# Layer 2 of an attention kernel in another order of slots

## The chip, the cores and the metric

The kernel runs on one core of a Trainium2 chip. The metric is the time of one execution on the device in microseconds (us). The engines are TensorE (PE in the profile; its weight loads PEld), VectorE (DVE), ScalarE (ACT), GpSimd (POOL) and SyncE (SP), which here only issues transfers.

## The reference

Input x has 8 batches of 512 rows by 512 columns, float32.

```python
x = layernorm(x + attention_1(x))       # q, k, v, o each with a low-rank adapter; rope; causal; 16 heads of 32
x = layernorm(x + ffn(x))
# ffn: a = attention_2(rmsnorm(x, ln1_w)); mod = 0.1 * tanh(a @ A); h = rmsnorm(x, ln2_w)
# gate = silu(h @ W_in.T + mod * (h @ A) @ B); out = x + (gate * (h @ W_up.T)) @ W_down.T
```

## The kernel before

The program has three parts, one behind the other: layer 1 (attention 1, to 788 us of the profiled execution), layer 2 (output projection of attention 1, residual, layer norm, RMS norm, attention 2 with values narrowed to 16 columns a head; 788 to about 1690 us), and the MLP. Products of float32 numbers are made of three passes over high and low parts ("split": ScalarE writes the high part, VectorE or GpSimd subtracts it for the low part).

Layer 2 goes through 8 batches; a batch has 4 group steps (g0 to g3) of 4 heads; a step has 12 slots, three for each head. In slot k of step g of batch b, each engine does its share of a fixed program, written out by hand:

- TensorE (`step`, L2142): the transposed scores of unit k (`score_t_unit`, L275 and L277), the probabilities times values of unit k-2 (`pv_unit`, L311), in slots 1 to 7 one or two score units of the next group for its row maxima (`score_unit`, L192), and then what the slot has in extras.
- ScalarE: two exponentials of unit k (`exp_unit`, L286, L287), copies of PSUM results, and the send of the shift row.
- VectorE: the low part of the probabilities of unit k-1 (`lo_unit`, L294, always first in the slot), the maxima (`score_max`, L206), in slot 7 `shift_split` (L217, L219), in slot 5 the reciprocal of the sums (`invert`, L1915), and extras.
- GpSimd: sums of the attention outputs (`merge` L1578, `weigh` L1584 to L1599), two of the four row tiles of h (`normalise_tile`, L1615), splits of the next attention output (`attn_chunk`, L1603).
- SyncE: gathers, stores, loads, and `stack_send` (L258, L262), twelve transfers for a group that bring q and k into the layout that the scores need.

`score_t_unit(k)` waits for `lo_done` of unit k-2, since its PSUM buffer has two halves. On VectorE that subtraction opens slot k-1.

The extras prepare batch b+1 during batch b. Their order: the output projection (`project_out`, L2067 and L2072, 52 matmuls, four tiles of rows, slots from `OUT_SLOTS` and `OUT_COUNT`) into the two halves of `lin_ps`; `add_residual` (L1846, with its statistics L1848); `variances` (L1855 to L1863), the roots by Newton steps (`root_start` L1307, `root_round` L1315 to L1319, `both_roots` L1875); `h_rows` for two tiles on VectorE (L1881) and two on GpSimd; `turn_h` on TensorE (L2083, four transpositions a tile), `h_tile` on ScalarE (L1697, L1698) and VectorE (L1891); q and k of group 0 (`project`, L2104, after `MADE_B`: for each group, for q and k, step, first and last slot, and where they leave PSUM), and so on. q and k of group 3 of batch b come in g1, of group 2 in g0. `h_times_a` (L2127) multiplies h with A in g1. `normalise_tile` on VectorE (L1886) makes x1 in `res`, `store_x1` (L1490) stores it. `load_x` (L1452) loads the next rows into `res`; `store_h` and `load` use the tile `wide` (named stage in the profile).

All waits are on semaphores with constants; each engine and each queue takes its instructions in order.

## Time and profile before

| | us |
|---|---|
| median of 3 runs | 2783.93 |
| lowest, highest | 2775.04, 2787.33 |
| profiled execution, own time | 2788.6 |
| its span | 2786.8 |
| mean granted TensorE clock, share of full speed | 0.98 |

The page gives the busy time of each engine and its share of the span. A view by stretches gives the same for chosen times. A timeline lists instructions in order of time, those of a kind and line merged, with the idle time of the engine before it and what ended that. A view of waits sums such idle times by who waited and who released. Line numbers are those of the kernel before. Durations overlap a little between instructions of one engine, so the distance from start to start is the better cost.

### The profile page before, as it was taken

Reading aid. Unit: us, or ns where it says so; the run is one execution under the profiler, and the core shown is the slowest. Engines: PE = TensorE matmul, PEld = TensorE weight load, DVE = VectorE, ACT = ScalarE, POOL = GpSimd, SP = SyncE. Lnnn points to the kernel's source line nnn. Section 1 sums busy time; section 2 is a strip of 40 time slices with the busy share of each in tenths; the row PEclk is TensorE's granted clock in tenths of the full one; section 3 lists DMA queues with packets and bytes.
Section 4 is the critical chain, followed back from the end, with each engine's and each line's share of the span. In section 5 each row is a group of like instructions: output and inputs, shape, how many; then the busy total and the mean of one; then the engine's idle time right before and its main releaser. Section 6 shows DMA issues by size and latency. Waiting matters only on the chain.

```text
span 2786.8 us, 40960 instructions
## 1 busy us (share of the span) xinstructions
PE 2629.9 (94%) x13584; PEld 2019.6 (72%) x13584; DVE 1600.0 (57%) x4341; ACT 1325.7 (48%) x2739; POOL 667.9 (24%) x535
## 2 busy tenths in 40 slices
PE   6999999999888999999999889999999999999998
PEld 5777777777566666666666647888888888888886
DVE  5777777777847788787787774222222423333333
ACT  3777777777734666666666674111111321111111
POOL 4556555556321322222222221000000000000000
PEclk9999999999889999999999979999999999999999
DMA  6565556665545664565554534111111311111100
GB/s 148 113 146 138 138 124 142 147 144 130 148 120 125 133 131 106 132 132 102 127 132 103 125 83 161 47 47 47 47 47 47 115 47 47 47 47 47 47 30 30
DMA packets 174634, 276.44 MB, mean 99 GB/s; under 512 B 29556, under 2 KB 53876, under 8 KB 173940
## 3 DMA queue, kind: packets, MB, share of 16 engines
q1 hardware_dynamic: 170884, 259.98, 39.1%
q0 software_dynamic: 2304, 12.58, 1.3%
q10 hardware_dynamic: 1264, 1.64, 0.2%
q8 instruction: 90, 1.47, 0.2%
q14 instruction: 92, 0.75, 0.1%
HBM read 97.03 MB, written 42.99 MB: 50 GB/s over the span
## 4 chain that ended last, share of the span: by engine, by line
PE 54%; DVE 9%; issue 3%; ACT 2%; DMA 2%; SPq 1%; POOL 0%; ACTq 0%; DVEq 0%; POOLq 0%
PE lin_ps L2575 13%; PE b_scores_ps L2586 13%; PE b_pv_ps L2556 6%; PE b_scores_t_ps L2556 6%; PE lin_ps L2104 5%; PE b_pv_ps L311 2%; DVE b_prob L294 2%; DVE b_junk L206 2%; PE b_scores_t_ps L275 2%; PE lin_ps L2067 2%; PE b_scores_ps L192 1%; DMA b_k_stack<-b_k_split 1%; PE lin_ps L2581 1%; PE b_scores_ps L2049 1%; SPq L262 1%
## 5 line engine op out<-in xcount | busy, mean ns | idle before, releaser
L286 ACT ACTIVATE b_prob<-b_scores_t_ps 128x384 fp32r<-128x384 f32 (+1 forms) x384 | 201.1, 524 | 218.1 <-PE b_scores_t_ps L277 198.9
L294 DVE TENSOR_TENSOR a_prob<-a_scores_t_ps,a_prob 128x384 fp32r<-128x384 f32 (+1 forms) x384 | 225.3, 593 | 135.7 <-ACT a_scores_t_ps L287 134.2
L294 DVE TENSOR_TENSOR b_prob<-b_scores_t_ps,b_prob 128x384 fp32r<-128x384 f32 (+1 forms) x384 | 225.8, 592 | 100.1 <-ACT b_scores_t_ps L287 100.0
L286 ACT ACTIVATE a_prob<-a_scores_t_ps 128x384 fp32r<-128x384 f32 (+1 forms) x384 | 201.7, 525 | 156.4 <-PE a_scores_t_ps L277 130.8
L311 PE MATMUL b_pv_ps<-b_prob,b_value 128*33 128x512 f32 (+3 forms) x1024 | 273.6, 336 | 0.1
L311 PE MATMUL a_pv_ps<-a_prob,a_value 128*65 128x512 f32 (+3 forms) x1024 | 271.1, 333 | 0.4 <-DVE a_prob L294 0.2
L206 DVE CUSTOM_DVE_ANT_0 b_junk<-b_scores_ps,spare 128x512 bf16<-128x512 f32 (+3 forms) x512 | 226.8, 483 | 66.3 <-PE b_scores_ps L192 63.8
L206 DVE CUSTOM_DVE_ANT_0 a_junk<-a_scores_ps,spare 128x512 bf16<-128x512 f32 (+3 forms) x512 | 226.6, 483 | 26.9 <-PE a_scores_ps L192 24.8
L2519 DVE TENSOR_TENSOR res<-b_scores_ps,b_first_gate 128x512 f32<-128x512 f32 x64 | 44.3, 692 | 331.9 <-PE b_scores_ps L2586 331.9
L2519 DVE TENSOR_TENSOR stage<-b_scores_ps,b_junk 128x512 f32<-128x512 f32 x64 | 44.3, 692 | 328.2 <-PE b_scores_ps L2586 328.2
L1143 PE MATMUL lin_ps<-x_split,w_split 128*128 128x512 f32 x768 | 216.7, 397 | 1.5 <-DVE w_split L938 1.2
L275 PE MATMUL b_scores_t_ps<-b_q_stack,b_k_stack 114*128 114x512 f32 (+3 forms) x512 | 157.4, 349 | 51.4 <-DVE b_prob L294 50.0
L2104 PE MATMUL lin_ps<-b_h_split,w_split 128*128 128x512 f32 x768 | 203.5, 401 | 1.7 <-ACT b_h_split L1698 1.2
L287 ACT ACTIVATE a_scores_t_ps<-a_scores_t_ps 128x384 f32<-128x384 f32 (+1 forms) x384 | 201.7, 525 | 0.0
L287 ACT ACTIVATE b_scores_t_ps<-b_scores_t_ps 128x384 f32<-128x384 f32 (+1 forms) x384 | 200.7, 523 | 0.0
L275 PE MATMUL a_scores_t_ps<-a_q_stack,a_k_stack 114*128 114x512 f32 (+3 forms) x512 | 151.9, 338 | 36.4 <-DVE a_prob L294 32.3
L275 PEld LDWEIGHTS b_scores_t_ps<-b_q_stack,b_k_stack 114*128 114x128 f32 x512 | 94.1, 195 | 109.2 <-DVE b_prob L294 92.0
L2104 PEld LDWEIGHTS lin_ps<-b_h_split,w_split 128*128 128x128 f32 x768 | 142.2, 191 | 36.4 <-ACT b_h_split L1698 1.6
L1143 PEld LDWEIGHTS lin_ps<-x_split,w_split 128*128 128x128 f32 x768 | 139.5, 190 | 31.3 <-DVE w_split L938 2.1
L2439 ACT ACTIVATE b_junk<-lin_ps 128x512 f32<-128x512 f32 x64 | 38.2, 597 | 243.6 <-PE lin_ps L2581 243.6
L2439 ACT ACTIVATE b_first_gate<-lin_ps 128x512 f32<-128x512 f32 x64 | 38.3, 598 | 241.5 <-PE lin_ps L2581 241.5
L275 PEld LDWEIGHTS a_scores_t_ps<-a_q_stack,a_k_stack 114*128 114x128 f32 x512 | 91.6, 193 | 83.3 <-DVE a_prob L294 66.7
(318 smaller groups left out, 5908.8 us busy)
## 6 DMA issues: line engine op xcount, KB each, us to landing
a_q_stack<-a_q_split SPq DMA_DIRECT2D x192, 128.0 KB, 3.4
a_k_stack<-a_k_split SPq DMA_DIRECT2D x192, 128.0 KB, 3.5
b_q_stack<-b_q_split SPq DMA_DIRECT2D x192, 128.0 KB, 3.1
b_k_stack<-b_k_split SPq DMA_DIRECT2D x192, 128.0 KB, 3.7
spare<-h_t SPq DMA_DIRECT2D x16, 1024.0 KB, 6.2
stage<-in_x_t SPq DMA_DIRECT2D x8, 1024.0 KB, 6.5
a_sum_hi<-a_pv_raw SPq DMA_DIRECT2D x32, 256.0 KB, 3.8
a_inverse_all<-softmax_sums SPq DMA_DIRECT2D x32, 256.0 KB, 3.5
```

Of the source, the lines that this page charges most:

```text
L206: last = dve.tensor_tensor_reduce(at.junk[:, k % 2, col:col + width], at.scores_ps[:, k % 2, col:col + width], rowmask[:, SEQ - width:SEQ] ...
L275: pe.matmul(at.scores_t_ps[:, k % 2, col:col + width], key[0:STACK_ROWS, h, kt * P:kt * P + P], q[0:STACK_ROWS, h, kt * P:SEQ], start=(i = ...
L286: act.activation(at.prob_hi[:, k % at.ring, 0:w], at.scores_t_ps[:, k % 2, 0:w], ACT.Exp, scale=SCALE)
L287: act.activation(at.scores_t_ps[:, k % 2, 0:w], at.scores_t_ps[:, k % 2, 0:w], ACT.Exp, scale=SCALE).then_inc(at.exp_done, 1)
L294: dve.tensor_tensor(at.prob_lo[:, k % at.ring, 0:w], at.scores_t_ps[:, k % 2, 0:w], at.prob_hi[:, k % at.ring, 0:w], ALU.subtract).then_in ...
L311: mm = pe.matmul(at.pv_ps[0:at.vcols, h % 2, kt * P:SEQ], at.value[:, kt, g * GH + h, :], prob[:, k % at.ring, col:col + width], start=(kt ...
L1143: mm = pe.matmul(lin_ps[:, bank, :], w_split[i][:, w, c, g * P:g * P + P], x_split[:, a, c, :], start=(x == 0), stop=False)
L2104: mm = pe.matmul(lin_ps[:, i, :], qk_split[i][:, w, c, g * P:g * P + P], h_split[:, a, c, :], start=(x == 0), stop=(x == 3 * KC - 1))
L2519: dve.tensor_tensor(self.product[bank], self.up_ps[:, bank, :], self.gate[bank], ALU.mult).then_inc(self.product_done, 1)
L2556: mm = pe.matmul(self.down_ps[t], self.product_split[kt % 2][:, a, t * P:t * P + P], self.w_down[kt][:, w, :], start=(kt == 0 and i == 0), ...
L2575: pe.matmul(self.gate_ps[:, bank, :], self.w_in_up[ft][:, w, c * 2 * P:c * 2 * P + P], self.h_split[run.pair][:, a, c, :], start=(c == 0 a ...
L2586: mm = pe.matmul(self.up_ps[:, bank, :], self.w_in_up[ft][:, w, c * 2 * P + P:(c + 1) * 2 * P], self.h_split[run.pair][:, a, c, :], start= ...
```

## The change

Layer 2: the fourth group's q and k are made in g1:3 to g1:6 (before g1:1 to g1:4). The four output tiles are made from g0:7 to g1:2 without a pause (before g0:7 to g1:0 and g1:5 to g1:8). The residuals are added in g0:9, g0:11, g1:1 and g1:3, their statistics in a function of its own one slot later, before the maxima. The second root is taken from the variance directly, so three small operations on VectorE go (a reciprocal, a product and `both_roots`) and the two additions no longer follow one another. Variances come in g1:4, roots in g1:5 and g1:6, row tiles in g1:6 and g1:8; GpSimd's two at the end of its g1. Transposition is in g1:9 to g2:0 (before g2:1 to g2:4), the next batch's q and k for group 0 in g2:2 to g2:5 (before g2:6 to g2:8), `h_times_a` in g1:8 and g1:9 (before g1:10 and g1:11). x1 is made in g3:6 to g3:9 (before g2:8 to g2:11) and stored at the end of SyncE's g3 (before: right behind its first gather).

Start of layer 1: the low part of the third weight moves from GpSimd to VectorE; ScalarE splits it before it copies the first projection; the sends of the adapter rows move from ScalarE's queue to SyncE's, behind the weights' loads.

```diff
@@ -662,6 +662,9 @@
                     sp.dma_start(w_stage[n][c], w[:, c, :]).then_inc(w_in[n], 16)
                 if n == 1:
                     constants()
+            sp.wait_ge(rows_zeroed, 2)
+            send_b(0)
+            send_low(0)
             for pair in range(2):
                 stack_send(sp, at, 0, 0, pair)
             for pair in range(2):
@@ -754,12 +758,6 @@
                     for tile in leaving(b, g, slot):
                         rope(*tile)
 
-            pool.wait_ge(w_ready, 2 * KC)
-            for c in range(KC):
-                pool.wait_ge(w_hi, 2 * KC + c + 1)
-                pool.tensor_tensor(w_split[2][:, 1, c, :], w_stage[2][c], w_split[2][:, 0, c, :],
-                                   ALU.subtract).then_inc(w_ready, 1)
-            pool.wait_ge(const_in, 80)
             for i in range(2):
                 rope(0, 1, i)
             for i in range(2):
@@ -876,21 +874,12 @@
             for c in range(KC):
                 x_chunk(0, c)
             adapter(0)
-            act.wait_ge(rows_zeroed, 2)
-            act.wait_ge(ab_ready, 2)
-            for r, part in enumerate((0, 1, 0)):
-                act.dma_start(b_stack[RANK * r:RANK * (r + 1), :, :].bitcast(F32),
-                              b_split[:, part, :].bitcast(F32)).then_inc(b_stacked, 16)
             weights(0)
             low(0)
-            weights(1)
-            act.wait_ge(low_ready, 1)
-            for r, part in enumerate((0, 0, 1)):
-                act.dma_start(low_stack[RANK * r:RANK * (r + 1), :, :].bitcast(F32),
-                              low_split[:, part, :].bitcast(F32)).then_inc(low_stacked, 16)
+            for n in range(1, 3):
+                weights(n)
             for i in range(2):
                 projected(0, 0, i)
-            weights(2)
             for i in range(2):
                 rotated_hi(0, 0, i)
             for i in range(2):
@@ -1063,6 +1052,7 @@
             low(0)
             weights(1)
             constants()
+            weights(2)
             for i in range(2):
                 exchange(0, 0, i)
                 first_rope(i)
@@ -1250,11 +1240,11 @@
 
 
 
-MADE_B = (((-2, 6, 8, -2, 8), (-2, 6, 9, -2, 9)), ((-3, 10, 12, -2, 3), (-2, 0, 2, -2, 4)),
-          ((-2, 3, 5, -2, 5), (-2, 5, 7, -2, 7)), ((-2, 1, 3, -2, 3), (-2, 3, 5, -2, 5)))
-OUT_SLOTS = (7, 5)
-OUT_COUNT = (6, 4)
-H_LO = 2
+MADE_B = (((-2, 2, 4, -2, 4), (-2, 4, 6, -2, 6)), ((-3, 10, 12, -2, 3), (-2, 0, 2, -2, 4)),
+          ((-2, 3, 5, -2, 5), (-2, 5, 7, -2, 7)), ((-2, 3, 5, -2, 5), (-2, 5, 7, -2, 7)))
+OUT_SLOTS = (7, -1)
+OUT_COUNT = (4, 4)
+TURN_SLOTS = (9, 10, 11, 12)
 VALUE_SLOTS = (5, 8)
 
 
@@ -1283,6 +1273,13 @@
         at = g * UNITS + slot - n * UNITS - OUT_SLOTS[n]
         if 0 <= at < OUT_COUNT[n]:
             yield from range(n * half + share(half, OUT_COUNT[n], at).start, n * half + share(half, OUT_COUNT[n], at).stop)
+
+
+def turned(b, g, slot):
+
+    for t in range(TT):
+        if (g - 1) * UNITS + slot == TURN_SLOTS[t] and not is_last(b):
+            yield t
 
 
 def gate_value_items(b, g, slot):
@@ -1515,8 +1512,6 @@
                     mlp.load_h(sp, mlp.start, 0)
                 if not first:
                     gather(*group(b, g, -1))
-                if g == 3 and not last:
-                    store_x1(b + 1)
                 if g == 2 and not last:
                     for t in range(TT):
                         store_h(b + 1, t)
@@ -1539,6 +1534,8 @@
                     store_z(b - 1)
                 if not (last and g >= 2):
                     stack_send(sp, at, *group(b, g, 2), 1)
+                if g == 3 and not last:
+                    store_x1(b + 1)
 
             sp.dma_start(wv_stage[:, :, :], wv).then_inc(wv_in, 16)
             sp.dma_start(sel[:, :], selector).then_inc(const_in, 16)
@@ -1631,9 +1628,6 @@
 
             def body(b):
                 for g in range(GROUPS):
-                    if g == 2 and has(b, 1):
-                        for t in range(2, TT):
-                            normalise_tile(b + 1, t)
                     if is_last(b) and g == 0:
                         pool.wait_ge(x1_out, BATCH * 16)
                         pool.wait_ge(h_out, BATCH * TT * 16)
@@ -1652,6 +1646,9 @@
                         adapter(b + 2)
                     if not (isinstance(b, int) and b == 0 and g == 0):
                         weigh(*group(b, g, -1))
+                    if g == 1 and has(b, 1):
+                        for t in range(2, TT):
+                            normalise_tile(b + 1, t)
 
             batches(pool, body, 2)
             for k in range(2, 4):
@@ -1771,7 +1768,7 @@
                             tanh(b - 1)
                         if slot == 4:
                             z_part(b - 1)
-                    if g == 2 and slot == 0:
+                    if g == 1 and slot == 10:
                         h_times_a(b)
                     if last and g == 1 and 5 <= slot < 6 + KC:
                         act.wait_ge(o_made, BATCH * TT)
@@ -1783,8 +1780,8 @@
                         mlp.low_b_hi(act)
                     if last and g == 3 and 5 <= slot < 5 + KC:
                         mlp.input_hi(act, mlp.start, slot - 5)
-                    if g == 2 and 2 <= slot < 6 and not last:
-                        h_tile(b + 1, slot - 2)
+                    for t in turned(b, g, slot - 1):
+                        h_tile(b + 1, t)
                     for to in left_b(b, g, slot):
                         projected(*to)
 
@@ -1844,6 +1841,8 @@
                 dve.wait_ge(o_made, b * TT + t + 1)
                 at_least(dve, in_done[1], b * 16)
                 dve.tensor_tensor(res[:, t, :], lin_ps[:, t % 2, :], res[:, t, :], ALU.add).then_inc(o_added, 1)
+
+            def statistics(b, t):
                 dve.wait_ge(o_added, b * TT + t + 1)
                 dve.bn_stats(stats[:, t, :], res[:, t, :]).then_inc(stats_done, 1)
 
@@ -1855,24 +1854,16 @@
                     dve.bn_aggr(mean_var[:, t, :], stats[:, t, :]).then_inc(ln_step, 1)
                 dve.wait_ge(ln_step, done + TT)
                 dve.tensor_scalar(squares[:, 0, :], mean_var[:, :, 1], LN_EPS, None, ALU.add).then_inc(ln_step, 1)
-                dve.wait_ge(ln_step, done + TT + 1)
-                dve.reciprocal(newton[:, 0, :], squares[:, 0, :]).then_inc(ln_step, 1)
-                dve.wait_ge(ln_step, done + TT + 2)
-                dve.tensor_tensor(newton[:, 1, :], newton[:, 0, :], mean_var[:, :, 1], ALU.mult).then_inc(ln_step, 1)
-                dve.wait_ge(ln_step, done + TT + 3)
-                dve.tensor_scalar(squares[:, 1, :], newton[:, 1, :], RMS_EPS, None, ALU.add).then_inc(ln_step, 1)
+                dve.tensor_scalar(squares[:, 1, :], mean_var[:, :, 1], 1.0 + RMS_EPS, LN_EPS * RMS_EPS, ALU.mult,
+                                  ALU.add).then_inc(ln_step, 1)
 
             def root_start(b):
-                done = b * LN_STEPS + TT + 4
+                done = b * LN_STEPS + TT + 2
                 dve.wait_ge(ln_step, done)
                 rsqrt_start(dve, ln_step, done, inv_root[:, :, :], squares[:, :, :], newton[:, :, :])
 
             def root_round(b, i):
-                rsqrt_round(dve, ln_step, b * LN_STEPS + TT + 4, inv_root[:, :, :], squares[:, :, :], newton[:, :, :], i)
-
-            def both_roots(b):
-                dve.wait_ge(ln_step, b * LN_STEPS + TT + 4 + RSQRT_STEPS)
-                dve.tensor_tensor(inv_root[:, 1, :], inv_root[:, 0, :], inv_root[:, 1, :], ALU.mult).then_inc(ln_step, 1)
+                rsqrt_round(dve, ln_step, b * LN_STEPS + TT + 2, inv_root[:, :, :], squares[:, :, :], newton[:, :, :], i)
 
             def h_rows(b, t):
                 if t == 0:
@@ -1929,12 +1920,14 @@
                 zero = isinstance(b, int) and b == 0
                 first = zero and g == 0
                 for slot in range(UNITS):
-                    if g == 1 and slot == 10 and not last:
-                        variances(b + 1)
                     if slot > 0:
                         lo_unit(dve, at, b, g, slot - 1)
                     elif not first:
                         lo_unit(dve, at, *group(b, g, -1), UNITS - 1)
+                    if g == 0 and slot == 10 and not last:
+                        statistics(b + 1, 0)
+                    if g == 1 and slot in (0, 2, 4) and not last:
+                        statistics(b + 1, 1 + (0, 2, 4).index(slot))
                     if not (last and g == GROUPS - 1):
                         for k in score_share(slot):
                             score_max(dve, at, rowmask, *group(b, g, 1), k)
@@ -1956,19 +1949,21 @@
                             z_term(b - 1)
                         if slot == 5:
                             z_part(b - 1)
-                    if g == 0 and slot == 10 and not last:
-                        add_residual(b + 1, 0)
+                    if g == 0 and slot in (9, 11) and not last:
+                        add_residual(b + 1, (9, 11).index(slot))
                     if g == 1 and not last:
-                        if slot in (1, 7, 9):
-                            add_residual(b + 1, 1 + (1, 7, 9).index(slot))
-                        if slot == 10:
+                        if slot in (1, 3):
+                            add_residual(b + 1, 2 + (1, 3).index(slot))
+                        if slot == 4:
+                            variances(b + 1)
+                        if slot == 5:
                             root_start(b + 1)
                             root_round(b + 1, 0)
-                        if slot == 11:
+                        if slot == 6:
                             for i in range(1, 3):
                                 root_round(b + 1, i)
-                            both_roots(b + 1)
                             h_rows(b + 1, 0)
+                        if slot == 8:
                             h_rows(b + 1, 1)
                     if last and g == 1 and 6 <= slot < 7 + KC:
                         mlp.weights_lo(dve, 0, slot - 6)
@@ -1978,22 +1973,21 @@
                         mlp.low_b_lo(dve)
                     if last and g == 3 and 6 <= slot < 6 + KC:
                         mlp.input_lo(dve, mlp.start, slot - 6)
-                    if g == 2 and not last:
-                        if slot >= UNITS - TT:
-                            normalise_tile(b + 1, slot - (UNITS - TT))
-                        if H_LO <= slot < H_LO + TT:
-                            h_tile(b + 1, slot - H_LO)
+                    for t in turned(b, g, slot - 1):
+                        h_tile(b + 1, t)
                     if slot > 0:
                         for to in left_b(b, g, slot - 1):
                             projected(*to)
+                    if g == 3 and 6 <= slot < 6 + TT and not last:
+                        normalise_tile(b + 1, slot - 6)
 
             for t in range(TT):
                 add_residual(0, t)
+                statistics(0, t)
             variances(0)
             root_start(0)
             for i in range(3):
                 root_round(0, i)
-            both_roots(0)
             dve.wait_ge(vw_made, 2)
             for t in range(2):
                 h_rows(0, t)
@@ -2056,10 +2050,10 @@
                 for x in items:
                     t, y = divmod(x, 3 * KC + 1)
                     bank = t % 2
-                    if y == 0 and not (isinstance(b, int) and b == 0):
-                        pe.wait_ge(qk_ready[bank], b * GROUPS - 1 + t // 2)
-                    elif y == 0 and t >= 2:
+                    if y == 0 and t >= 2:
                         pe.wait_ge(o_added, b * TT + t - 1)
+                    elif y == 0 and not (isinstance(b, int) and b == 0):
+                        pe.wait_ge(qk_ready[bank], b * GROUPS - 1)
                     if y < 3 * KC and b == 0 and t < 2:
                         continue
                     if y < 3 * KC:
@@ -2077,8 +2071,10 @@
                 pe.wait_ge(*((h_ready, b * 2 + t + 1) if t < 2 else (h_late, b * 2 + t - 1)))
                 if t >= 2:
                     pe.wait_ge(h_hi, b * TT + t - 1)
+                elif isinstance(b, int) and b == 0:
+                    pe.wait_ge(o_added, 3 + t)
                 else:
-                    pe.wait_ge(o_added, b * TT + 3 + t)
+                    pe.wait_ge(qk_ready[bank], b * GROUPS)
                 for c in range(KC):
                     mm = pe.transpose(lin_ps[:, bank, c * P:c * P + P], wide[:, t, c * P:c * P + P], eye[:, :].bitcast(F32))
                 mm.then_inc(h_turned, 1)
@@ -2095,7 +2091,7 @@
                         elif g == 2:
                             pe.wait_ge(at.value_ready, b * 3 + 3)
                         elif g == 3 and not is_last(b):
-                            pe.wait_ge(o_added, (b + 1) * TT + 1 + i)
+                            pe.wait_ge(o_added, (b + 1) * TT + 3 + i)
                         else:
                             pe.wait_ge(qk_ready[i], number(b, g))
                     (w, a), c = HI_FIRST[x // KC], x % KC
@@ -2166,10 +2162,10 @@
                         modulation(b - 1)
                     if g < 2 and not last:
                         project_out(b + 1, out_items(g, slot))
-                    if g == 1 and slot in (10, 11):
-                        h_times_a(b, share(3 * KC, 2, slot - 10))
-                    if g == 2 and 1 <= slot < 5 and not last:
-                        turn_h(b + 1, slot - 1)
+                    if g == 1 and slot in (8, 9):
+                        h_times_a(b, share(3 * KC, 2, slot - 8))
+                    for t in turned(b, g, slot):
+                        turn_h(b + 1, t)
                     if g == 3 and slot in (8, 9) and has(b, 2):
                         low(b + 2, share(3 * KC, 2, slot - 8))
                     for to in made_b(b, g, slot):
```

## Rows read from the trace of the kernel before

**Rows 1.** The page, part 1: busy time, share of the span, instructions.
```profile
PE 2629.9 (94%) x13584; PEld 2019.6 (72%) x13584; DVE 1600.0 (57%) x4341; ACT 1325.7 (48%) x2739; POOL 667.9 (24%) x535
```
**Rows 2.** View by stretches, batch 3, steps g1 and g2: stretch, its length, busy.
```profile
1188.30:1216.60 28.30, 27.61 (x151) 19.76 (x150) 23.82 (x76) 15.87 (x33) 3.23 (x3) 1.00 0.38 78
1216.60:1242.60 26.00, 22.74 (x134) 16.75 (x132) 23.16 (x62) 18.72 (x40) 8.73 (x5) 1.00 0.60 142
```
**Rows 3.** Waits in 1188.3 to 1242.6: waiter, releaser, total, times, longest.
```profile
PE b_scores_t_ps L275 <- DVE b_prob L294: 3.9, 6, 1.4
```
**Rows 4.** Timeline of TensorE, batch 3: start, duration, what, idle before.
```profile
1206.62 1.54 PE L2067 MATMUL lin_ps<-w_split,x_split 128*128 128x512 f32 x6
1208.00 0.34 PE L275 MATMUL b_scores_t_ps<-b_q_stack,b_k_stack 114*128 114x256 f32 x2
...
1210.71 0.50 PE L275 MATMUL b_scores_t_ps<-b_q_stack,b_k_stack 114*128 114x512 f32 x1
...
1220.12 0.42 PE L275 MATMUL b_scores_t_ps<-b_q_stack,b_k_stack 114*128 114x256 f32 x2
...
1236.87 0.45 PE L275 MATMUL b_scores_t_ps<-b_q_stack,b_k_stack 114*128 114x512 f32 x1
```
**Rows 5.** Timeline of VectorE, batch 3, g1:3 to g1:11.
```profile
1195.29 0.55 DVE L294 TENSOR_TENSOR b_prob<-b_scores_t_ps,b_prob 128x384 fp32r<-128x384 f32 x1
...
1207.79 0.87 DVE L217 TENSOR_SCALAR b_shift<-b_rowmax 128x16 fp32r<-128x16 f32 x1
...
1208.78 0.68 DVE L1846 TENSOR_TENSOR res<-lin_ps,res 128x512 f32<-128x512 f32 x1
1209.50 0.69 DVE L1848 BATCH_NORM_STATS2 b_stats<-res 128x6 f32<-128x512 f32 x1
1210.11 1.00 DVE L294 TENSOR_TENSOR b_prob<-b_scores_t_ps,b_prob 128x384 fp32r<-128x384 f32 x2
...
1214.18 0.16 DVE L1307 TENSOR_SCALAR b_newton<-b_squares 128x8 int32<-128x8 int32 x1
...
1215.53 0.16 DVE L1315 TENSOR_TENSOR b_newton<-b_inv_root 128x8 f32<-128x8 f32 x1
...
1217.01 1.29 DVE L1881 TENSOR_SCALAR stage<-res,b_mean_var,b_inv_root 128x512 f32<-128x512 f32 x2
```
**Rows 6.** Timeline of GpSimd, batch 3, g1 and g2.
```profile
1207.34 1.28 POOL L1584 TENSOR_TENSOR b_late<-b_late 64x512 f32<-64x512 f32 x1 [9.20 <-DMA b_late<-softmax_sums]
...
1217.01 4.39 POOL L1615 TENSOR_SCALAR stage<-res,b_mean_var,b_inv_root 128x512 f32<-128x512 f32 x2 [7.67 <-DVE b_inv_root L1875]
```
**Rows 7.** Timeline of ScalarE, batch 3: first exponentials of g2:2 and g2:5.
```profile
1220.71 0.49 ACT L286 ACTIVATE b_prob<-b_scores_t_ps 128x384 fp32r<-128x384 f32 x1
...
1226.72 0.49 ACT L286 ACTIVATE b_prob<-b_scores_t_ps 128x384 fp32r<-128x384 f32 x1
```
**Rows 8.** Timeline of TensorE, two idle times, then the stretch behind the second.
```profile
1218.82 0.44 PE L275 MATMUL b_scores_t_ps<-b_q_stack,b_k_stack 114*128 114x384 f32 x1 [1.41 <-DVE b_prob L294]
...
1560.24 0.49 PE L192 MATMUL b_scores_ps<-b_k_stack,b_q_stack 112*128 112x512 f32 x1 [1.84 <-DMA b_k_stack<-b_k_split]
...
1560.70:1564.10 3.40, 3.40 (x12) 2.78 (x11) 1.17 (x3) 0.68 (x2) 0.00 (x0) 0.50 0.78 146
```
**Rows 9.** Waits in 856 to 1580: TensorE for the stacks.
```profile
PE b_scores_ps L192 <- DMA b_k_stack<-b_k_split: 8.4, 7, 2.4
```
**Rows 10.** Issues, us to landing, first behind 1 MB, then not; g0:6, g0:7 start.
```profile
b_q_stack<-b_q_split SPq DMA_DIRECT2D x3, 128.0 KB, 6.2
...
b_q_stack<-b_q_split SPq DMA_DIRECT2D x3, 128.0 KB, 3.2
...
1176.96 0.49 DVE L294 TENSOR_TENSOR b_prob<-b_scores_t_ps,b_prob 128x384 fp32r<-128x384 f32 x1
...
1179.13 0.34 PE L275 MATMUL b_scores_t_ps<-b_q_stack,b_k_stack 114*128 114x384 f32 x1
```
**Rows 11.** Timelines at the starts of layer 1 and layer 2.
```profile
29.35 1.78 DVE L1001 TENSOR_TENSOR a_rope_turned<-a_rope_turned,res 128x512 f32<-128x512 f32 x1
...
815.99 0.66 PE L2083 MATMUL lin_ps<-eye,stage 128*128 128x128 f32 x4 [2.29 <-DVE stage L1881]
```

3 lines of the change are left out of this document (2 added, 1 removed).

## The prediction

> Slots: "g1:5" is slot 5 (one unit of exponentials) of group step 1 of a batch in layer 2; a slot starts on TensorE with its first L275 matmul and on VectorE with its L294 subtraction, which belongs to the slot before. All times of a standard batch are those of batch 3, whose steps g1 and g2 run from 1188.3 to 1242.6 us.
>
> **What bounds the kernel now.** I read the page first: TensorE is busy 94% of the span and nothing else is near it [rows 1]. So a reordering can pay only by removing TensorE's idle time or lose by adding some. Next the busy time by stretch: in g1 VectorE is busy 23.8 of 28.3 us and in g2 23.2 of 26.0 us while TensorE still idles 3.3 us in g2 [rows 2]. In these two steps VectorE is nearly as full as TensorE. Third, the waits of the stretch: what TensorE waits for there is VectorE's `b_prob` subtraction, L294, and nothing else of size [rows 3]. The rule behind it is in the code and can be checked in the timeline: slot k on TensorE needs the L294 that opens VectorE's slot k-1, so TensorE's start is VectorE's previous slot start plus 0.6 us. VectorE opens g1:8 at 1210.11 and TensorE g1:9 at 1210.71; at g2:1, 1218.82, the wait is 1.41 us and the row names its releaser [rows 4, 5, 8]. Where VectorE is more than a slot behind, it sets the pace.
>
> **The change, part by part.**
>
> (a) Output tiles earlier. All 52 matmuls of the output projection are now done by the end of g1:2; before, 38 of that sort were (26 of the output, 12 of group 3's q). Six of these take 1.38 us (1206.62 to 1208.00) [rows 4], so one is 0.22 us at most; 14 more make about 2.8 us. TensorE therefore reaches g1:3 2.8 us later and VectorE, which waits there for score rows that TensorE makes, 2.6 us later. TensorE has lighter slots behind that (g1:7 loses its 6 matmuls), so that by its own work it would open g1:9 only 0.9 us later, and that with six of the `h_times_a` matmuls already done.
>
> (b) VectorE in g1:3 to g1:7, the step that decides. Before, these five slots take 1195.29 to 1210.11, 14.8 us [rows 5]. Added: one residual tile (0.61, taken like the statistics row's neighbour), the variances without the reciprocal's chain (0.65, estimated from four aggregates and two small operations at 0.2 apart), root start and first round (0.9: 1214.18 to the next L294), two rounds (1.2 of the 1.5 us from 1215.53 to 1217.01; the product of both roots is gone), one row tile (0.5 of 1.29 for two). Removed: residual and statistics that stood in g1:7 (1.33, from 1208.78 to 1210.11), group 3's k subtraction pushed to g1:8 (0.61), a wait for scores (0.4). Statistics of tile 3 take 0.61 [rows 5]. The sum is 14.8 + 0.6 + 0.6 + 0.65 + 0.9 + 1.2 + 0.5 - 1.33 - 0.6 - 0.4 = 16.9. In it is one collision: the L217 in g1:7 takes 0.87 us, while instructions as small take 0.17 beside it, and ends at 1208.66, as GpSimd's L1584 ends at 1208.62 [rows 5, 6]. Without it the stretch is 16.2; if the new rounds meet GpSimd's two instructions instead, 17.5. So VectorE opens g1:8 at 1210.1 + 2.6 + (1.4 to 2.7) = 1214.1 to 1215.4, and g1:7 1.95 before that. TensorE needs that for g1:8, then 2.4 us of work: g1:9 at 1215.2 to 1216.5 instead of 1210.71: 4.5 to 5.8 us late. TensorE stands idle for 3 to 4 us in one piece before g1:8.
>
> (c) Transposition. ScalarE needs 2.0 us for a slot with two copies of a turned tile (three slots take 1220.71 to 1226.72) [rows 7]. The four slots g1:10 to g2:1 hold the four tiles, `h_times_a`'s copy and a copy of the PV result: 2.2 + 2.2 + 1.9 + 1.7 = 8.1 us on ScalarE, while TensorE has 4.6 us of work in them (columns at the rate of rows 4, and 0.2 a slot); VectorE's subtraction waits for each copy, and TensorE for VectorE. It comes out at 10.85 us from g1:9 to g2:2, against 9.4 before (1210.71 to 1220.12) [rows 4]: 1.4 late. Before, the same ScalarE-bound slots stood at g2:2 to g2:5, beside score maxima that now come later; moving them saves nothing by itself.
>
> (d) g2:2 to g2:9. Next batch's q and k (24 matmuls, 5.2 us) fill slots that VectorE bounded before. TensorE's own sum, made the same way, is 13.0 us; VectorE's reciprocal, q subtraction, maxima, shift and k subtraction in g2:5 to g2:7 leave it waiting again for about 2 us, 3.3 with a GpSimd collision. 15.1 to 16.3 us against 16.75 (1220.12 to 1236.87) [rows 4]: 1.6 to 0.4 gained.
>
> (e) Waits for stacks. q and k three slots sooner put their copies on SP's queue some 4 us before g3:1 needs them. The waits of TensorE for them over seven batches are 8.4 us, and two of them were followed by a slow stretch of the clock: 1.7 us gained per batch [rows 9]. Group 3's stacks are issued later (its q and k leave at g1:5 and g1:7) but are needed only at g2:1.
>
> (f) SP. `store_x1` (1 MB) moves from behind g3's gather to before the next g0's. A transfer right behind a 1 MB one lands after 6.2 us instead of 3.2 [rows 10]; the gather and the reciprocal behind it in g0:5 then come about 2 us later. VectorE opens g0:6 at 1176.96, and TensorE could start g0:7 from 1177.6 but starts at 1179.13 [rows 10]: 1.6 us in hand, so 0 to 0.5 lost.
>
> (g) VectorE's x1 normalisations go to g3:6 to g3:9, where GpSimd splits the next attention chunks; TensorE is heavy at g3:8 and g3:9, which hides them (0 to 0.2; 1.2 each if that cover were gone). GpSimd's row tiles are done 2 us before g1:11 turns them. Nothing.
>
> (h) The clock. Where TensorE was idle for 1.84 us the granted clock fell to half (1.2 GHz) for 3.4 us; after 1.41 us it did not [rows 8]. The 3 to 4 us before g1:8 are longer than any idle stretch of the layer, and the half-speed piece costs 1.7 us of the full slots g1:8 and g1:9. I take 1.2 per batch.
>
> (i) Starts. In layer 1 GpSimd's third weight split goes to VectorE. VectorE's rope product took 1.78 us beside it, where 0.61 is usual; losing about 4 us of such stretching against 2.4 of new subtractions and copies queued ahead gives 2 us (bounds 4 gained, 1 lost: if the stacks' sends, now behind the weights on SP's queue, land late). Layer 2 starts with TensorE waiting 2.29 us for the row statistics [rows 11]; the chain loses four dependent steps, 0.8 us.
>
> **A rule of the skill.** L1881 on VectorE beside L1615 on GpSimd: both start at 1217.01, and VectorE's two take 1.29 us while GpSimd's take 4.39, so neither held the other to its end [rows 5, 6]; L217 was held [rows 5]. The Trainium skill, "SBUF — State Buffer", section "Who interferes with whom", says that a VectorE instruction in a two-port mode or with two SBUF inputs is blocked for the whole of a GpSimd instruction that reads SBUF. By that rule the shift of g1:7, beside a row tile of 2.2 us, would wait 1.2 us or more. The L217 row agrees with it, the L1881 rows don't.
>
> **The sum.** Per batch, with 0.4 off because batch 3's g1:8 was a short one: (4.1 to 5.4) + 1.4 - (0.4 to 1.6) - 1.7 + (0 to 0.5) = 2.2 to 5.2, taken 3.7, plus 1.2 for the clock: 4.9. Seven batches carry it (the last prepares nothing): 34, less 1.5 in the first, which lacks `z_term` and `z_part` on VectorE (estimated at a row operation each), less 3 at the starts: +30. The profiled execution's own time is 2788.6 us (span 2786.8), 4.7 above the median of 2783.9. So 2818.6 there, 2814 as a median. With all lower ends it is +9, with all upper ends +47.
>
> **Rivals.** (1) VectorE keeps up. If it is not over a slot behind at g1:7 (it decides: lag under 1 us at g1:5, where I get 1.3), TensorE goes by its own work: 3.9 us less from g0:7 to g3:0, 1.7 at the stacks, seven times, and 3 at the starts: -42, 2742 us. For it: TensorE's 94%; against: 16 us of VectorE work beside 10.6 us of TensorE work. (2) No change: the lull is given back in g2, where TensorE's work now stands where VectorE has room, and the clock holds: 0 to +12, 2784 to 2796. (3) SP's order costs more: the gather lands 3.3 us late in every g0 and all of it shows: 23 more, 2837. (4) GpSimd holds VectorE in g1:7 by its row tiles, 1.2 to 2.3 per batch: 2822 to 2830. (5) The order isn't what the slots say, for instance if waits on `o_added` hold TensorE in g1:3; I see none that does.
>
> **Chances.** Forecast 0.55, (1) 0.13, (2) 0.17, (3) 0.08, (4) 0.07. Half a per cent, 14 us, is about what a measurement tells from no change. Faster 0.13, same 0.17, slower 0.70. The range reaches into (2) and a little below, and to (3): 2776 to 2832.
>
> **What will show it.** Right: VectorE's L294 opens g1:8 some 17 us after g1:3; an idle of TensorE of 3 us or more before an L275 in g1, and half clock after it; L192's waits for DMA gone from g3; steps g1 and g2 together about 6 us longer than their 54 [rows 2] and a batch about 5. Wrong if g1 is no longer than before, or if the largest wait stands in g0 or g3.

## The result, and the profile of the changed kernel

The changed kernel takes 2838.8 us (median; 2836.2 to 2845.6), the one before 2784.6: a ratio of 1.0205, 95% interval 1.019 to 1.022. It is slower, as forecast, but by 54 us where 30 were forecast, and above the upper end of the range, 2832. Its profiled execution took 2836.8 us with a span of 2835.0.

The page and the view by stretches, with the first seven batches of layer 2 of both kernels (columns: stretch, length, busy time and count of TensorE, weight loads, VectorE, ScalarE and GpSimd, granted clock, DMA share, GB/s). The first fence is the changed kernel, the second the one before:

```profile
PE 2661.3 (94%) x13584; PEld 2030.5 (72%) x13584; DVE 1589.5 (56%) x4321; ACT 1326.5 (47%) x2739; POOL 657.5 (23%) x531
...
842.40:1636.00 793.60, 715.17 (x3887) 509.03 (x3886) 566.75 (x1653) 468.40 (x1003) 174.67 (x143) 0.95 0.49 109
```
```profile
855.40:1581.40 726.00, 675.51 (x3887) 493.50 (x3885) 573.68 (x1674) 468.19 (x1003) 178.32 (x143) 1.00 0.55 120
```

The page alone misleads: TensorE is 94% busy as before [rows 1]. The stretch shows why. The seven batches take 67.6 us more. The same 3887 matmuls keep TensorE busy 39.7 us longer, at a mean granted clock of 0.95 instead of 1.00, and only the other 28 us are idle time. The rest goes the other way: layer 2's first unit opens at 842.4 instead of 855.4 us (13 sooner), and the last batch's four steps are 6.4 us shorter. 67.6 - 13.0 - 6.4 = 48.2, the difference of the two spans.

By step, mean of batches 1 to 5, in us (unit starts of the timeline, and the time at half clock in them):

| | before: length, half clock, idle | after: length, half clock, idle |
|---|---|---|
| g0 | 23.5, 0.0, 0.8 | 28.0, 0.7, 2.0 |
| g1 | 28.6, 0.0, 1.0 | 34.5, 5.5, 5.1 |
| g2 | 26.1, 0.0, 3.3 | 27.2, 6.1, 3.0 |
| g3 | 26.0, 0.7, 2.0 | 24.8, 0.0, 1.0 |
| batch | 104.1, 0.7, 7.1 | 114.5, 12.3, 11.1 |

Of g0's 4.5 us more, 2.3 are work: 11 more output matmuls stand in it, which g1 no longer has.

The waits of TensorE in layer 2's first seven batches (waiter, releaser, total, times, longest), changed kernel:

```profile
PE b_scores_t_ps L275 <- DVE b_prob L294: 56.8, 73, 3.9
PE b_scores_ps L229 <- DVE b_shift L219: 6.9, 7, 1.4
PE lin_ps L2079 <- ACT b_h_split L1695: 6.5, 7, 0.9
...
PE b_scores_ps L192 <- DMA b_k_stack<-b_k_split: 0.4, 1, 0.4
```

The wait for the stacks of [rows 9] is gone, 8.4 to 0.4 us. The wait for L294 stands there instead, up to 3.9 us long. Batch 3 shows where. First VectorE's slots from g1:3 to g1:8 (the openings of g1:3, g1:6, g1:7 and g1:8; timeline as in [rows 5]), then TensorE from g1:8:

```profile
1217.28 0.55 DVE L294 TENSOR_TENSOR b_prob<-b_scores_t_ps,b_prob 128x384 fp32r<-128x384 f32 x1
...
1227.47 0.55 DVE L294 TENSOR_TENSOR b_prob<-b_scores_t_ps,b_prob 128x384 fp32r<-128x384 f32 x1
...
1231.43 0.68 DVE L294 TENSOR_TENSOR b_prob<-b_scores_t_ps,b_prob 128x512 fp32r<-128x512 f32 x1
...
1233.60 0.55 DVE L294 TENSOR_TENSOR b_prob<-b_scores_t_ps,b_prob 128x384 fp32r<-128x384 f32 x1
```
```profile
1232.16 0.45 PE L275 MATMUL b_scores_t_ps<-b_q_stack,b_k_stack 114*128 114x256 f32 x2 [2.37 <-DVE b_prob L294]
...
1233.19 2.60 PE L2123 MATMUL b_scores_ps<-b_h_split,b_low_a_split 128*16 128x512 f32 x6
...
1236.02 0.73 PE L275 MATMUL b_scores_t_ps<-b_q_stack,b_k_stack 114*128 114x512 f32 x1
...
1247.22 0.45 PE L275 MATMUL b_scores_t_ps<-b_q_stack,b_k_stack 114*128 114x256 f32 x2 [0.97 <-DVE b_prob L294]
```

The stretch behind it:

```profile
1233.40:1236.80 3.40, 3.40 (x13) 1.60 (x12) 2.67 (x6) 0.74 (x2) 3.40 (x2) 0.50 0.40 85
```

And GpSimd's row tiles, which begin beside g1:7's score maxima:

```profile
1232.69 4.30 POOL L1612 TENSOR_SCALAR stage<-res,b_mean_var,b_inv_root 128x512 f32<-128x512 f32 x2
```

VectorE needs 16.3 us for the five slots that took 14.8 before [rows 5]. TensorE stands idle for 2.37 us and gets half clock for 3.4 us right behind; g1:9 opens 26.0 us after g1 began, where it was 22.4 [rows 4]. This is one of the mildest batches: the idle before g1:8 is 2.2, 3.3, 3.9, 2.4, 3.9, 2.4 and 3.3 us in batches 0 to 6. These three sizes go with what VectorE's row tile and Newton steps met on the way. In batches 0, 3 and 5 they met nothing that held them. In batches 1 and 6 the row tile L1872 met GpSimd's sum, here in batch 1:

```profile
999.35 1.49 DVE L1872 TENSOR_SCALAR stage<-res,b_mean_var,b_inv_root 128x512 f32<-128x512 f32 x1
```
```profile
999.29 1.26 POOL L1581 TENSOR_TENSOR b_late<-b_late 64x512 f32<-64x512 f32 x1 [10.04 <-DMA b_late<-softmax_sums]
```

L1872 takes 1.49 us where it takes 0.55 in batch 3. In batches 2 and 4 it was the last Newton step that met the sum (and L1872 behind it took 1.05 us), here in batch 4:

```profile
1342.44 0.17 DVE L1314 SCALAR_TENSOR_TENSOR b_newton<-b_newton,b_squares 128x8 f32<-128x8 f32 x1
1342.64 1.19 DVE L1316 SCALAR_TENSOR_TENSOR b_inv_root<-b_newton,b_inv_root 128x8 f32<-128x8 f32 x1
```
```profile
1342.55 1.25 POOL L1581 TENSOR_TENSOR b_late<-b_late 64x512 f32<-64x512 f32 x1 [9.73 <-DMA b_late<-softmax_sums]
```

L1316 takes 1.19 us instead of 0.17 and ends as L1581 does. The rule of the Trainium skill weighed in the prediction ("SBUF — State Buffer", "Who interferes with whom") fits this row, as it fitted L217. The row tile of batch 1 was held too, but ended 0.29 us after L1581; the L1881 rows [rows 5, 6], of the same form, still speak against it.

The second place is g0. The store of x1, the gather of the sums behind it on SP's queue (in us: issue, landing, from the trace's issues) and VectorE's reciprocal, mean of batches 1 to 6 from the start of g0: the sums land at 13.4 instead of 10.8, the reciprocal opens at 13.4 instead of 11.3, TensorE g0:7 at 15.5 instead of 14.2 and g0:8 at 18.9 instead of 16.2. Half of the sums' lateness is in the issue (at 9.0 instead of 7.6, behind the store's and with longer issues), half in the landing (4.4 us after the issue instead of 3.1). VectorE in g0 of batch 3, which begins at 1182.7:

```profile
1195.59 0.94 DVE L1906 RECIPROCAL b_inverse<-b_sums 16x128 f32<-16x128 f32 x1 [1.57 <-DMA b_sums<-b_pv_raw]
...
1201.01 1.07 DVE L217 TENSOR_SCALAR b_shift<-b_rowmax 128x16 fp32r<-128x16 f32 x1
```

The store was issued at 1188.8 and landed at 1194.4, the sums, issued at 1191.6, landed at 1195.6.

### The profile page after: what moved, and what is told of

The parts are those of the page before. It is cut to its first block, busy times and chain, and to the rows that moved or that the text cites. A ratio compares the mean times of both kernels' runs of the same rounds, so it can differ in the third digit from the quotient of the medians.

```text
span 2835.0 us, 40935 instructions
## 1 busy us (share of the span) xinstructions
PE 2661.3 (94%) x13584; PEld 2030.5 (72%) x13584; DVE 1589.5 (56%) x4321; ACT 1326.5 (47%) x2739; POOL 657.5 (23%) x531
## 3 DMA queue, kind: packets, MB, share of 16 engines
q1 hardware_dynamic: 171508, 260.57, 38.3%
q10 hardware_dynamic: 640, 1.05, 0.2%
## 4 chain that ended last, share of the span: by engine, by line
PE 54%; DVE 7%; issue 3%; SPq 3%; ACT 2%; DMA 2%; POOL 0%; DVEq 0%; ACTq 0%; POOLq 0%
PE lin_ps L2571 13%; PE b_scores_ps L2582 13%; PE b_pv_ps L2552 6%; PE b_scores_t_ps L2552 6%; PE lin_ps L2061 3%; PE lin_ps L2100 3%; PE b_pv_ps L311 3%; DVE b_junk L206 2%; PE b_scores_t_ps L275 2%; DVE b_prob L294 1%; DMA b_sums<-b_pv_raw 1%; PE b_scores_ps L192 1%; PE lin_ps L2577 1%; PE b_scores_ps L2123 1%; SPq L262 1%
## 5 line engine op out<-in xcount | busy, mean ns | idle before, releaser
L294 DVE TENSOR_TENSOR a_prob<-a_scores_t_ps,a_prob 128x384 fp32r<-128x384 f32 (+1 forms) x384 | 225.3, 593 | 135.0 <-ACT a_scores_t_ps L287 133.3
L294 DVE TENSOR_TENSOR b_prob<-b_scores_t_ps,b_prob 128x384 fp32r<-128x384 f32 (+1 forms) x384 | 227.8, 595 | 123.1 <-ACT b_scores_t_ps L287 122.7
L311 PE MATMUL b_pv_ps<-b_prob,b_value 128*33 128x512 f32 (+3 forms) x1024 | 280.9, 344 | 0.1
L275 PE MATMUL b_scores_t_ps<-b_q_stack,b_k_stack 114*128 114x512 f32 (+3 forms) x512 | 163.8, 362 | 69.9 <-DVE b_prob L294 67.6
L2435 ACT ACTIVATE b_junk<-lin_ps 128x512 f32<-128x512 f32 x64 | 38.3, 598 | 244.1 <-PE lin_ps L2577 244.1
L2435 ACT ACTIVATE b_first_gate<-lin_ps 128x512 f32<-128x512 f32 x64 | 38.3, 599 | 241.5 <-PE lin_ps L2577 241.5
```

Source lines behind the costliest of these rows:

```text
L275: pe.matmul(at.scores_t_ps[:, k % 2, col:col + width], key[0:STACK_ROWS, h, kt * P:kt * P + P], q[0:STACK_ROWS, h, kt * P:SEQ], start=(i = ...
L294: dve.tensor_tensor(at.prob_lo[:, k % at.ring, 0:w], at.scores_t_ps[:, k % 2, 0:w], at.prob_hi[:, k % at.ring, 0:w], ALU.subtract).then_in ...
L311: mm = pe.matmul(at.pv_ps[0:at.vcols, h % 2, kt * P:SEQ], at.value[:, kt, g * GH + h, :], prob[:, k % at.ring, col:col + width], start=(kt ...
```

## The experiments

All compare with the kernel before on the same chip (its median 2782.8, 2784.5 and 2785.0 us in the three groups of runs). The changed kernel was measured only in the group of the result, so a difference to it carries some 1 to 2 us between groups. "Half clock" is the sum over layer 2's batches 0 to 6; it is 78 us in the changed kernel and 7 before.

**1. The starts alone.** The kernel before, with layer 1's start and the shorter statistics of the change.

```
+            sp.wait_ge(rows_zeroed, 2)
+            send_b(0)
+            send_low(0)
...
-                pool.tensor_tensor(w_split[2][:, 1, c, :], w_stage[2][c], w_split[2][:, 0, c, :], ...
+            weights(2)
...
+                dve.tensor_scalar(squares[:, 1, :], mean_var[:, :, 1], 1.0 + RMS_EPS, LN_EPS * RMS_EPS, ...
```

> The kernel before with two parts of the change alone: layer 1's start (the third weight's low part on VectorE, the stack sends on SP) and the shorter statistics (two tensor_scalars in place of the chain with a reciprocal, no product of the roots). Layer 2's order stays the old one. Theory (these two make the whole of the earlier start of layer 2, and nothing else does): layer 1's first unit opens 4.3 us sooner, layer 2's first unit 13 us sooner (842 instead of 855), and a batch of layer 2 keeps its 103 to 104 us: about 13 us less, 2772. Rival (the prediction's step i): 3 us less, and what was seen beyond that in the changed kernel is chance of a single profile: 2781. Second rival (the shorter statistics relieve VectorE in g1 as well): a batch shrinks by up to 1 us more, 2765.

Measured 2774.5 us, 0.9977 (0.996 to 0.9993). Run a second time it was to serve as the comparison of experiment 7:

> The kernel before with layer 1's start and the shorter statistics alone, once more, as the comparison for the run beside it. Theory: 0.9975 of before, 2777 us, and the first unit of layer 2 again 5 to 6 us sooner than the 855.4 of before, which makes 5 to 7 us of the 13 that the changed kernel showed; the other half is scatter of single profiles in layer 1. Rival: 842, the whole 13.

Measured 2778.1 us, 0.9977 (0.9966 to 0.9988). Both together: 7 to 8 us. Layer 2 opens at 849.9 and 848.7, so 5.5 and 6.7 us sooner, and a batch takes 103.8 and 103.5 us against 104.1. The 13 us of the changed kernel's profile are not all the change's; in the twelve experiments, which all have this start, layer 2 opens between 844.3 and 849.9. What the part gives is seen in VectorE's rope products of layer 1's start, where [rows 11] had 1.78 us:

```profile
30.85 0.68 DVE L990 TENSOR_TENSOR a_rope_turned<-a_rope_turned,res 128x512 f32<-128x512 f32 x1
31.57 0.69 DVE L993 TENSOR_TENSOR res<-res,a_rope_turned 128x512 f32<-128x512 f32 x1
```

Two tiles have two such products each, three of the four took 1.66 to 1.78 us beside GpSimd's third weight, and the values' matmuls follow at 34.3 (35.3 in the second run) instead of 38.3 us.

**2. x1 back.** The changed kernel with normalisations and store of x1 at their old places.

```
                     gather(*group(b, g, -1))
+                if g == 3 and not last:
+                    store_x1(b + 1)
...
                     stack_send(sp, at, *group(b, g, 2), 1)
-                if g == 3 and not last:
-                    store_x1(b + 1)
...
+                    if g == 2 and slot >= UNITS - TT and not last:
+                        normalise_tile(b + 1, slot - (UNITS - TT))
...
-                    if g == 3 and 6 <= slot < 6 + TT and not last:
-                        normalise_tile(b + 1, slot - 6)
```

> The changed kernel with the x1 normalisations back at g2:8 to g2:11 and the store of x1 back behind g3's gather (as before the change); all else as changed. Theory (the gather of g0 waits behind the 1 MB store): VectorE's reciprocal of g0:5 waits for nothing, g0:6 and g0:7 take 2.3 us less together, g0's idle time falls from 2.0 to about 0.9 us, and a batch shrinks by 1.2 to 2.3 us: 10 to 16 us less than the changed kernel, 2823 to 2829. Rival (g0's extra 4.5 us are TensorE's own 11 more output matmuls, and the gather's lateness is hidden by them): under 3 us in all, 2836 to 2841.

Measured 2828.0 us, 1.0163 (1.0141 to 1.0186): 10.8 less than the changed kernel. In its profile g0 falls from 28.0 to 25.9 us, the idle in it from 2.0 to 0.9, a batch by 2.8. The late gather is a loss of its own, the one that the prediction had as rival (3). The edit moves the normalisations with the store, and the half clock falls too, from 78 to 61 us, so the 10.8 us are not the gather's alone; the part that shows in g0 is.

**3. The chain behind the output tiles at its old place.**

```
-MADE_B = (((-2, 2, 4, -2, 4), (-2, 4, 6, -2, 6)), ...
+MADE_B = (((-2, 6, 8, -2, 8), (-2, 6, 9, -2, 9)), ...
-TURN_SLOTS = (9, 10, 11, 12)
+TURN_SLOTS = (13, 14, 15, 16)
-                        if slot == 4:
+                        if slot == 9:
                             variances(b + 1)
-                        if slot == 5:
+                        if slot == 10:
                             root_start(b + 1)
...
```

> The changed kernel with its output tiles still in a row (g0:7 to g1:2) and group 3's q and k behind them, but with all that follows back at its old place: variances g1:9, roots and first round g1:10, two rounds and both row tiles g1:11, transposition g2:1 to g2:4, the next batch's q and k g2:6 to g2:8. Theory (the loss of g1 and g2 is the crowd on VectorE in g1:4 to g1:8, its idle of TensorE and the half clock behind it): the idle of 2.2 to 3.9 us before g1:8 is gone, half clock in g1 and g2 falls from 11.6 us a batch to under 2, g1 and g2 together come back from 61.8 to about 55, the stack waits at g3:1 return (1.7 a batch): 5 us less a batch, 2803. Rival (the output tiles in a row and group 3's q and k are what costs, by filling TensorE's queue ahead of VectorE's score rows): g1 stays above 32 us, 2830 or more.

Measured 2806.8 us, 1.0084 (1.0066 to 1.0103): 32 less. g1 falls from 34.5 to 27.0 us, the half clock from 78 to 31 us. What is left of it stands mostly in g2. There TensorE idles 1.96 to 1.97 us at g2:1 in all seven batches; half clock comes with it or right behind in batches 0, 1, 2 and 6, and not in 3, 4 and 5. Batch 3, the idle and the stretch around it:

```profile
1230.31 0.44 PE L275 MATMUL b_scores_t_ps<-b_q_stack,b_k_stack 114*128 114x384 f32 x1 [1.96 <-DVE b_prob L294]
```
```profile
1227.40:1234.40 7.00, 4.99 (x34) 3.82 (x35) 5.78 (x19) 5.18 (x12) 4.40 (x2) 1.00 0.73 128
```

**4. One Newton round.** Two of the three rounds left out of layer 2's inverse roots (so its row statistics are only roughly normalised).

```
                         if slot == 6:
-                            for i in range(1, 3):
-                                root_round(b + 1, i)
                             h_rows(b + 1, 0)
```

> The changed kernel with one Newton round of the inverse roots instead of three in layer 2 (two rounds, six small VectorE instructions in g1:6, are left out of the computation). Theory (each us of VectorE work in g1:4 to g1:7 is a us of TensorE's idle before g1:8): 1.2 us less work, the idle before g1:8 falls from 3.3 to about 2.1 us, and with half the half-clock time a batch shrinks by 1.2 to 3: 9 to 20 us less than the changed kernel, 2819 to 2830. Rival (what delays g1:8 is a collision with GpSimd or the copies on ScalarE, not VectorE's queue): under 3 us in all, 2835 or more.

Measured 2815.7 us, 1.0124 (1.0104 to 1.0144): 23 less for 8.4 us of VectorE work (1.2 us in each of seven batches), more than the theory's upper end. TensorE in batch 3 of this kernel, at g1:8:

```profile
1220.29 0.44 PE L275 MATMUL b_scores_t_ps<-b_q_stack,b_k_stack 114*128 114x256 f32 x2 [1.09 <-DVE b_prob L294]
```

The idle of 2.37 us is 1.09 here, and no half clock follows; in all there are 24 us of it instead of 78. The idle before g1:8 is 1.0 to 1.1 us in every batch: with the rounds the collisions with L1581 in the row tile and the Newton steps went too, so 2.0 us of idle go a batch, on average, for 1.2 us of work. A us of VectorE work in this place costs its own length and, by what it makes the rest meet and by the clock, more.

**5. Matmuls that nobody reads.** Ten extra matmuls of 512 columns ahead of g1:8, first into the bank of `lin_ps` that the transposition will use, then into a PV bank that is free.

```
+                    if g == 1 and slot == 8 and not last:
+                        pe.wait_ge(qk_ready[0], (b + 1) * GROUPS)
+                        for _ in range(10):
+                            pe.matmul(lin_ps[:, 0, :], qk_split[0][:, 0, 0, 0:P], h_split[:, 0, 0, :], ...
```

> The changed kernel with ten more matmuls of 512 columns (2.1 us at full clock, their result is never read) ahead of g1:8 in batches 0 to 6, where TensorE stands idle for 2.2 to 3.9 us. It does more work, and is late by what of it doesn't fit into the idle stretch. Theory (the clock is the term of the sum that was mis-sized: 78 us at half clock in the first seven batches cost some 36 us, of which g1's and part of g2's follow this idle stretch): the half-clock pieces behind g1:8 go, g1 shrinks by 2 us and g2 by 1 to 3: 15 to 30 us less than the changed kernel, 2809 to 2824. Rival (the half clock only runs where TensorE waits for VectorE anyway and costs nothing): the same as the changed kernel, 2838, or later by up to 7 us for the work that doesn't fit.

Measured 2848.2 us, 1.0237 (1.0214 to 1.026): 9 more, though its interval overlaps with that of the changed kernel (1.019 to 1.022), so the sign is not firmly shown. The theory was not tested, since the fillers themselves waited; VectorE's subtraction of q, for which they wait, was no sooner than what g1:8 waits for. TensorE in batch 3:

```profile
1240.80 3.59 PE L2147 MATMUL lin_ps<-b_h_split,w_split 128*128 128x512 f32 x10 [2.70 <-DVE b_q_split L1889]
1244.18 0.53 PE L275 MATMUL b_scores_t_ps<-b_q_stack,b_k_stack 114*128 114x256 f32 x2
```

They ran behind the idle, in part at half clock (3.59 us for ten), and delayed g1:8. The second form:

```
+                        pe.wait_ge(at.pv_copied, number(b, g) * GH + 1)
+                        for _ in range(10):
+                            pe.matmul(at.pv_ps[:, 0, :], qk_split[0][:, 0, 0, 0:P], h_split[:, 0, 0, :], ...
```

> The changed kernel with ten more matmuls of 512 columns ahead of g1:8 (batches 0 to 6), this time into the PV bank that is free there, so that they wait for nothing; in the first such kernel they waited for VectorE's subtraction of group 3's q, TensorE stood idle 1.8 us before them and was late by them, and the half clock stayed at 61 us. Theory (half clock costs time): the idle before g1:8 falls from 3.3 us a batch to about 1.2, half clock in g1 and g2 falls from 11.6 us a batch to about half, a batch shrinks by 2 to 3 us: 14 to 21 us less than the changed kernel, 2818 to 2825. Rival (VectorE sets the pace in these slots at either clock, and half clock is no loss there): 2835 to 2842, with the half-clock pieces gone all the same.

```profile
1222.18 2.49 PE L2147 MATMUL b_pv_ps<-b_h_split,w_split 128*128 128x512 f32 x10
1225.55 0.45 PE L275 MATMUL b_scores_t_ps<-b_q_stack,b_k_stack 114*128 114x256 f32 x2 [0.88 <-DVE b_prob L294]
...
1226.58 1.55 PE L2124 MATMUL b_scores_ps<-b_h_split,b_low_a_split 128*16 128x512 f32 x6
```

The view by stretches of its batches 0 to 6:

```profile
848.70:1617.90 769.20, 708.28 (x3958) 507.96 (x3956) 563.30 (x1653) 467.39 (x1003) 175.20 (x143) 0.99 0.51 112
```

Measured 2822.9 us, 1.0149 (1.0126 to 1.0172): 16 less than the changed kernel, with 70 matmuls more. The idle before g1:8 is broken up (0.88 left in batch 3, 0 to 1.6 in the others), the six matmuls of `h_times_a` behind it take 1.55 us where they took 2.60, half clock in g1 and g2 falls from 11.6 to 1.4 us a batch. The mean clock is 0.99. g1:8 opens no sooner (23.2 us after g1's start in both kernels, mean of batches 1 to 5), but g1:9 opens 1.7 us sooner and g3 3.7, counted from g1's start. No other engine has less to do, so the gain is the clock's: 16 us, or 2.3 a batch, with the fillers' own cost already taken off.

**6. Both repairs, and the same with fillers.** Output tiles in a row, group 3's q and k, `h_times_a` two slots sooner (g1:8 and g1:9), GpSimd's row tiles in its g1 and the shorter statistics are then what is left of the change in layer 2.

> Both repairs together: the changed kernel with the chain behind the output tiles at its old place (alone 2807) and the x1 normalisations and store at theirs (alone 10.8 us less). What is left of the change in layer 2 is the output tiles in a row and group 3's q and k behind them. Theory (the two losses are independent): 2796, batches of 106.5 us. Rival (they overlap, since the late gather and the idle of g2 are made up by the same slack): 2801 to 2807. If the output tiles in a row were harmless by themselves, this would reach the 2775 of the starts alone; the theory says it stays 15 to 20 us above that.

Measured 2797.6 us, 1.0048 (1.0029 to 1.0066). The two losses add up (10.8 and 32.0 alone, 41.2 together); but it stays 20 us above the starts alone. In every one of the seven batches TensorE idles 1.95 to 1.97 us at g2:1 where it was 1.40 to 1.43 before [rows 8], and in every one half clock follows; before, in none. Batch 3, the idle and the stretch behind it:

```profile
1222.95 0.44 PE L275 MATMUL b_scores_t_ps<-b_q_stack,b_k_stack 114*128 114x384 f32 x1 [1.96 <-DVE b_prob L294]
```
```profile
1223.60:1227.00 3.40, 3.40 (x15) 2.86 (x15) 1.64 (x4) 2.57 (x6) 1.93 (x1) 0.50 0.55 79
```

A likely reason, not tested apart: TensorE has less to do just before g2:1, since the twelve matmuls of `h_times_a` left g1:10 and g1:11 and six of the output left g1:7, while VectorE's crowd in g1:10 and g1:11 stands where it stood. Six fillers ahead of g2:0:

```
+                    if g == 2 and slot == 0 and not last:
+                        pe.wait_ge(at.pv_copied, number(b, 1) * GH + 3)
+                        for _ in range(6):
+                            pe.matmul(at.pv_ps[:, 0, :], qk_split[0][:, 0, 0, 0:P], h_split[:, 0, 0, :], ...
```

> The kernel with the chain and x1 at their old places and only the output tiles in a row, plus six matmuls of 512 columns whose result is never read (1.3 us) ahead of g2:0, where each batch has an idle stretch of 1.96 us and 3.4 us of half clock behind it. Theory (its remaining 3.4 us a batch over the starts alone are 0.9 of longer idle and 1.7 to 2 of half clock): the half clock in g2 goes, a batch shrinks from 107.2 to about 105.5: 2783 to 2788. Rival (half clock in g2 is no loss, since VectorE and ScalarE set the pace there): 2796 or more.

```profile
1212.58 1.67 PE L2146 MATMUL b_pv_ps<-b_h_split,w_split 128*128 128x512 f32 x6 [0.22 <-ACT b_pv_raw L323]
...
1215.61 0.44 PE L275 MATMUL b_scores_t_ps<-b_q_stack,b_k_stack 114*128 114x384 f32 x1 [0.70 <-DVE b_prob L294]
```

Measured 2781.5 us, 0.9987 (0.9978 to 0.9996): 16 less than without the 42 useless matmuls, half clock 1 us instead of 31, a batch 105.0 us instead of 107.2.

**7. The chain half-way.** x1 back, and the same instructions two or three slots later than in the change, spread over more slots.

```
-                        if slot == 4:
+                        if slot == 6:
                             variances(b + 1)
-                        if slot == 5:
+                        if slot == 7:
                             root_start(b + 1)
                             root_round(b + 1, 0)
-                        if slot == 6:
+                        if slot == 8:
                             for i in range(1, 3):
                                 root_round(b + 1, i)
+                        if slot == 9:
                             h_rows(b + 1, 0)
-                        if slot == 8:
+                        if slot == 10:
                             h_rows(b + 1, 1)
...
-TURN_SLOTS = (9, 10, 11, 12)
+TURN_SLOTS = (11, 12, 13, 14)
```

with the next batch's q at g2:4 and its k at g2:6.

> The changed kernel with x1 back and the chain half-way: variances g1:6, roots and first round g1:7, two rounds g1:8, row tiles g1:9 and g1:10, transposition g1:11 to g2:2, next batch's q g2:4, k g2:6. q and k still leave before g2:9, so the stacks wait for nothing at g3:1. Theory (the loss is the crowd of VectorE work in g1:4 to g1:6 on top of score maxima, shift and q/k subtractions, and it goes when the same work stands behind g1:7): idle before g1:8 under 1 us, half clock under 3 us a batch, a batch of 105 to 106 us: 2785 to 2795, better than with the chain at its old place by the 1.7 us a batch of the stack waits. Rival (the crowd only moves to g1:9 to g2:1, where the transposition makes ScalarE the bound): 2800 to 2815.

Measured 2770.9 us, 0.9959 (0.9949 to 0.997), better than the theory's 2785 to 2795 and than both kernels. Beside the starts alone on one chip:

> The kernel with the chain half-way and x1 back once more, beside the starts alone on the same chip. Theory (beyond the starts, the chain half-way gains the stack waits of g3:1 and loses nothing): it stays at 0.996 of before, 2 to 5 us under the starts alone. Rival (its 3.7 us over the starts alone were between two jobs, not between two kernels): the two agree within 1 us.

Measured 2771.2 us, 0.995 (0.9936 to 0.9963), against 2778.1 and 0.9977 (0.9966 to 0.9988): the intervals don't touch, so this order is worth 7 us itself. The waits of TensorE and the stretch of batches 0 to 6 in the first run of this kernel:

```profile
PE b_scores_t_ps L275 <- DVE b_prob L294: 34.8, 68, 1.5
```
```profile
847.70:1565.80 718.10, 675.58 (x3887) 489.46 (x3886) 561.80 (x1653) 465.63 (x1003) 176.40 (x143) 1.00 0.55 122
```

The largest wait is 1.5 us, nothing waits for the stacks, the clock never falls in these batches, and a batch takes 103.2 us. The same with x1 as the change has it:

> The chain half-way as in the kernel that beats before, but with the x1 normalisations at g3:6 to g3:9 and the store of x1 behind everything else of g3 on SP, as the change has them. Theory (the late gather is a loss of its own, 1.6 to 2.1 us a batch, whatever the rest does): 2782 to 2787, g0 back to 27.5 to 28 us against 25.8. Rival (the loss in g0 only showed because VectorE came late out of g1 and g2 anyway): under 4 us, 2771 to 2775.

Measured 2783.8 us, 0.9993 (0.9984 to 1.0002): 12.6 more than with x1 back, g0 28.3 us instead of 25.8. So the late x1 costs 1.8 us a batch here, where TensorE hardly gets half clock (7 us with it, none without), and 1.5 in experiment 2.

## Why the prediction was right in direction and wrong in size

The step that failed is (f), the late gather, put at 0 to 0.5 us a batch and measured at 1.5 to 1.8; the term that was most mis-sized is (h), the clock. A third, smaller part is likely the collisions in (b).

**(a) Output tiles earlier: right.** TensorE reaches g1:3 2.9 us later, 2.3 in g0 and 0.6 in g1, where 2.8 was said.

**(b) VectorE in g1:3 to g1:7: right in the cause, a little small in size.** 16.3 us in batch 3, which met no collision, said 16.2; with collisions, said up to 17.5, it is 17.8 to 18.9 us, and four of seven batches (1, 2, 4 and 6) had them. Idle of 2.2 to 3.9 us before g1:8, said 3 to 4; without a collision it is 2.2 to 2.4. Experiments 3 and 4 show it to be the cause.

**(c) Transposition: right within 0.4.** g1:9 to g2:2 is 11.2 us, 1.8 more than before; 1.4 was said. L2079's wait for ScalarE's copy, 6.5 us over seven batches, is in it. (The four ScalarE slots of the prediction add up to 8.0, not 8.1.)

**(d) g2:2 to g2:9: 16.7 us on average,** 0.2 less than before where 0.4 to 1.6 was said. With the clock kept up (`filler_pv`) it is 15.8, inside what was said for batch 3. The clock ate it. So it did from g2:9 to g3:0, for which the sum has nothing: 6.4 us instead of 5.7, and 5.5 with the clock kept up.

**(e) Stacks: right.** 8.4 us of waiting became 0.4; g3:1 is 1.4 us shorter a batch, said 1.7.

**(f) SP's order: this step failed.** The lateness was sized well, 2.6 us where "about 2" was said. The error is in "1.6 us in hand, so 0 to 0.5 lost". Of 2.2 us that the reciprocal is late, the slack swallows part once: g0:7 opens 1.3 late. But the slack was VectorE's for the slots behind as well. VectorE is then late at g0:7 too, L217 there meets GpSimd's sum L1581 in every one of batches 1 to 6 (0.8 to 1.2 us), where it met the same sum (then L1584) in three of them before and took 0.17 in the others, and g0:8 opens 2.7 late, of which 0.46 is TensorE's own added work. The part costs 10.8 us by experiment 2 and 12.6 by experiment 7, where at most 3.5 was said. Rival (3) had the mechanism, with 23 us as its price beyond the forecast. That its 2837 us lies so near the measured 2838.8 is luck: the part cost half of that, and the clock made up the rest.

**(g) x1 on VectorE at g3:6 to g3:9: not shown apart.** g3 is 0.3 us (experiment 7) and 0.5 us (experiment 2) shorter with x1 back, which moves the store too: 0.5 at most, said 0 to 0.2.

**(h) The clock: the term that was mis-sized most.** Said: one piece of 3.4 us a batch, 1.2 us lost. Measured: 12.3 us at half clock a batch, 3.6 pieces. TensorE's busy time for the same matmuls grows by 39.7 us in seven batches, 5.7 each. Not all of that is loss, since part of it fills idle time; what was bought back by the fillers before g1:8 is 16 us, net of their own work, with 61 of the 78 us of half clock gone. Two things were missed. One idle stretch of 3 us was followed by one or two pieces of 3.4. And the later, shorter idle times fell too: a wait of 1.41 to 1.43 us before L229 in g2:8 (batches 0, 2, 4 and 6) was followed by half clock each time, where 1.41 in [rows 8] was not. "After 1.41 it did not" was taken from one place and used for all. 1.96 us at g2:1 went with half clock in seven of seven batches of experiment 6 and in four of seven of experiment 3, so the length of the idle alone doesn't decide. The Trainium skill ("TensorE: Matmul & The Clock Gate", section "HAM oscillation — how this bites in real kernels") warns of idle gaps longer than these; the measurement decides.

**(i) Starts: right in sign, too small.** 3 us said, 7 to 8 measured for the kernel with them and the shorter statistics of every batch. A rope product takes 0.69 us when nothing stretches it, not 0.61, and three of four were stretched.

**The sum.** Said per batch: 4.9. Measured: 67.6 / 7 = 9.7. With the fillers of `filler_pv`, so nearly without half clock, a batch is still (769.2 - 726.0) / 7 = 6.2 us longer than before. So 3.5 of the 9.7 went with the clock in the profiles (2.3 by the medians), where 1.2 was said. About 1.5 more is (f), and about 1 is left, for which the collisions of (b) are the likely cause. The split can't be made exact, since the clock falls because of the same idle times. The sum also has nothing for the last batch, which became 6.4 us shorter. Of the chances, 0.70 on slower stood on the right side. "Wrong if the largest wait stands in g0 or g3": it stood in g1, as said, yet g0 lost 2.2 us beyond its work. GpSimd's row tiles (rival 4) didn't hold the shift: L217 in g1:7 takes 0.3 to 0.6 us in batches 0 to 6, less than the 0.8 to 1.25 of before; it was the sum of L1581 that collided, with the row tile or a Newton step.

**Left open.** Why 1.41 to 1.43 us of idle before L229 is followed by half clock and 1.40 to 1.43 at g2:1 in the kernel before never is. In experiments 2, 4 and 5 (`x1_back`, `one_round`, `filler`, `filler_pv`) the same wait of 1.42 to 1.53 us went with it nine times and four times not. Nor is it known why 1.96 us at g2:1 did in only four of seven batches of experiment 3. In the last batch the two profiles differ by 6.4 us. Single profiles scatter there (83.4 to 94.7 us with the new start), but not at random: its g0 takes 21.3 to 21.9 us in the six kernels with the late x1 and 23.8 to 27.2 in the other eight, so the late x1 gives back 2 us or more there.

## What to carry to other kernels

Price an idle stretch on TensorE with the slow clock behind it: where a reordering gathers small waits into one of 2 us or more, look for the granted clock of every stretch behind it, and spread the other engine's work over more slots before giving up the reordering (54 us slower as made, 14 us faster, 7 of them by the start, with the same chain two or three slots later and x1 put back). Slack seen at one place can be spent only once: a queue that is 2 us late with 1.6 "in hand" also moves all that the late engine does next. And an engine's stretch of idle can be measured for its clock part by putting work there that waits for nothing.

## What the runs showed of the hardware

- Useless matmuls made the kernel faster twice: 70 of them by 16 us, 42 by 16 us, by keeping the granted clock at 2.4 GHz.
- An idle stretch of 1.95 to 1.97 us at g2:1 was followed by 3.4 us at 1.2 GHz in 7 of 7 batches of one kernel (`late_x1`), and went with 3.4 or 6.8 us of it in 4 of 7 of another (`chain_late`); one of 1.40 to 1.43 us at the same place in none of 7 (the kernel before).
- A VectorE instruction of 0.17 us took 1.19 us beside GpSimd's L1581, and ended with it, one of 0.55 us (the row tile L1872) 1.49 us; two row tiles of GpSimd (4.30 us) held VectorE's L217 only to 0.3 to 0.6 us.
